# Scan inputs: fp32 products replaced by three float32r products on split operands, the parts made by ScalarE and Pool

## The chip, the cores and the metric

The program runs on one core of one Trainium2 chip. The metric is the device time of one execution in microseconds. The kernel before takes 3812.51 us (median of 3 runs, 3805.7 to 3818.8). Engines are called by the names of the profile: PE is TensorE, ACT ScalarE, DVE VectorE, POOL GpSimd (Pool), SP SyncE.

## What is computed

A chain of four blocks over 4096 tokens of width 256: an attention, a mixture of experts, a selective scan and a quantised feed-forward. The change is in the stage that makes the scan's inputs. Cut to what it computes:

```python
xz = einsum('bld,de->ble', xn, w_in)               # 256 -> 1024
x_path, z_path = split(xz, 2, axis=-1)             # 512 and 512
x_path = silu(causal_conv4(x_path) + b_conv)       # called xc below
Bseq, Cseq = x_path @ w_b, x_path @ w_c            # 512 -> 16 each
delta = softplus(x_path @ w_delta + b_delta)       # 512 -> 512
# handed on: delta, delta * x_path, Bseq, Cseq, x_path, silu(z_path)
```

## The kernel before

Each block is a function with its own engine programs. The function here is `scan_inputs` (names begin with `si_` in the profile). It goes over 8 groups of 512 tokens (GN), channels on the partitions. For one group g:

- `product_xz`: PE makes 8 outputs n of 128 channels, each from 2 matmuls (k) of 128x128 weights and 512 columns, into three rotating banks `ps_xz`. ACT copies each out (`copy_xz`): n = 0 to 3 to `xp`, n = 4 to 7 to `z`. From n = 3 on a product waits for the copy three before it, because of the three banks.
- DVE convolves `xp` (`convolve`: 4 tap-0 operations and 12 multiply-adds of 512), ACT takes the sigmoid in three passes (`sigmoid_conv`), DVE multiplies (`make_xc`) to `xc`.
- `product_xc`: PE makes `ps_d` (4 outputs x 4 matmuls with `w_delta`) and `ps_bc` (4 matmuls with `w_bc`, 32 columns of weights).
- Softplus: ACT magnitudes (`magnitude`), DVE `positive` and `correction`, ACT `logarithm`, DVE `make_delta` (two operations) and `delta_x`.
- PE turns delta times x (`turn`), ACT copies it out (`copy_turned`), SP stores it. ACT and DVE also make the z gate (`sigmoid_z`, `make_zs`).

All engines run their own program in order and wait on semaphores. `run_stages(eng, GROUPS, (stage, behind), ...)` sets the order: in step s the engine runs each stage in the listed order for group s - behind. So a step of PE is `product_xc(s-1)`, `turn(s-2)`, `product_xz(s+1)`; a step of ACT is magnitudes(s-1), `copy_turned(s-2)`, `sigmoid_conv(s)`, `logarithm(s-1)`, `copy_xz(s+1)`, `store_bc(s-1)`, `sigmoid_z(s)`; one of DVE is `convolve(s)`, `halo(s+1)`, `make_zs(s-1)`, `positive(s-1)`, `correction(s-1)`, `make_xc(s)`, `make_delta(s-1)`, `delta_x(s-1)`. POOL has nothing in the stage but three memsets at its start.

Of the kernel before, what the change touches and what calls it, by code (L numbers as in the profile page):

```python
# [13 lines left out]
F32 = mybir.dt.float32  # L14
BF16 = mybir.dt.bfloat16
I32 = mybir.dt.int32
ALU = mybir.AluOpType
# [1729 lines left out]
def scan_inputs(nc, io, scratch):  # L1747
# [5 lines left out]
    with ExitStack() as ctx:  # L1753
        r = Room(nc, ctx, "si")
        w_in, w_delta = r.sb("w_in", [P, KC, 2 * DI]), r.sb("w_delta", [P, DT, DI])
        w_bc = r.sb("w_bc", [P, DT, 2 * NS])
# [3 lines left out]
        xn_t = r.sb("xn_t", [P, 2, KC, GN])  # L1760
        xp, z = r.sb("xp", [P, DT, HALO + GN]), r.sb("z", [P, 2, DT, GN])
        conv, sig_c, sig_z = (r.sb(n, [P, DT, GN]) for n in ("conv", "sig_c", "sig_z"))
        xc, zs = r.sb("xc", [P, 2, DT, GN]), r.sb("zs", [P, DT, GN])
        mag, one_e, log, pos = (r.sb(n, [P, DT, GN]) for n in ("mag", "one_e", "log", "pos"))
        val = r.sb("val", [P, 2, 2, DT, GN])
        dx_t, b_t = r.sb("dx_t", [P, DT, GT, P]), r.sb("b_t", [P, GT, 2 * NS])
        bc = r.sb("bc", [2 * NS, GN])
        XZ = 3
# [5 lines left out]
                 "corr_ready", "log_ready", "sum_ready", "delta_ready", "dx_ready", "dx_turned", "dx_copied", "bc_turned", "b_copied",  # L1774
                 "bc_ready", "bc_copied", "xc_stored", "zs_stored", "delta_stored", "dx_stored", "b_stored", "bc_stored")
# [6 lines left out]
        with nc.Block() as block:  # L1782
            @block.sync
            def _(sp):
                sp.dma_start(w_in[:, :, :], io["w_in"].rearrange("(k p) e -> p k e", p=P)).then_inc(s["loaded"], 16)
# [10 lines left out]
                def load(g, slot):  # L1796
                    if third_on(g):
                        sp.wait_ge(s["xz_ready"], (g - 1) * 2 * DT)
                    sp.dma_start(xn_t[:, slot, :, :], tiles(scratch.xn_t, g)).then_inc(xn_loaded[slot], 16)

                def store_zs(g, slot):
                    sp.wait_ge(s["zs_ready"], g + 1)
                    sp.dma_start(tiles(scratch.zs, g), zs[:, :, :]).then_inc(s["zs_stored"], 16)
# [5 lines left out]
                def store_delta(g, slot):  # L1809
                    sp.wait_ge(s["delta_ready"], g + 1)  # L1810
                    sp.dma_start(tiles(scratch.delta, g), val[:, slot, 0, :, :]).then_inc(s["delta_stored"], 16)
# [20 lines left out]

            @block.vector
            def _(dve):
                CONV = DT * TAPS - 1
                dve.wait_ge(s["loaded"], 4 * 16)
                dve.wait_ge(s["keep_set"], 3)
# [59 lines left out]
                def make_delta(g, slot):  # L1897
# [3 lines left out]
                    dve.tensor_tensor(log[:, :, :], log[:, :, :], mag[:, :, :], ALU.subtract).then_inc(s["sum_ready"], 1)  # L1901
# [1048 lines left out]
```

## Time and profile before

| | |
|---|---|
| runs, median | 3812.51 us |
| profiled execution, its own time | 3818.61 us |
| its span | 3816.9 us |
| stage `scan_inputs` in it | about 2335 to 2675 us of the span |
| busy in that stage (340 us) | PE 282.22, DVE 223.19, ACT 204.42, POOL 1.96 us |

Times of rows are counted in microseconds from the start of the span. One plain fp32 matmul of the program stands in the trace as two MATMUL records (256 records of `si_w_in` for 128 matmuls). A wait in brackets is idle time of that engine just before the row, and what ended it. PEclk is the clock that TensorE was granted (1.0 is 2.4 GHz, 0.5 is 1.2 GHz).

### The profile page before, as it was taken

To read this page: it belongs to the slowest core of one execution; us is meant where nothing else is said; L and a number is where in the kernel's file an instruction comes from. 1 tells how busy PE (TensorE), PEld (TensorE's weight loads), DVE (VectorE), ACT (ScalarE), POOL (GpSimd) and SP (SyncE) were. 2 spreads that over 40 slices of the span, in tenths; PEclk is the share of its full clock that TensorE was granted. 3 is DMA by queue.
4 is the path that set the end of the run, shared out by engine and by line. 5 is a ranking of instruction groups with operands and counts; after the bars stand their busy time and mean duration, and the time that the engine had idled before them with its cause. 6 is when DMAs were issued, how large, how long until landed. Compare 5 with 4: busy or idle time off the path is not lost. (4 is left out here: it accounts for less than half of the span.)

```text
span 3816.9 us, 87664 instructions
## 1 busy us (share of the span) xinstructions
PE 3298.5 (86%) x34938; PEld 1884.3 (49%) x34939; DVE 2927.6 (77%) x4552; ACT 2057.6 (54%) x2972; POOL 1173.3 (31%) x910
## 2 busy tenths in 40 slices
PE   4769999999999999968699775997799999747876
PEld 1433333333333333326466552343687787546665
DVE  5659999998999999706344254676699999868986
ACT  0316777776777777833011155665565766334553
POOL 0100000000000000005100270000799999747775
PEclk8868999998999999967899866998899999879998
DMA  1674023030303120043222253333543434211110
GB/s 55 220 187 47 13 42 46 8 48 6 48 4 49 20 34 5 5 154 118 79 65 64 75 160 117 112 124 133 138 132 116 133 116 134 90 57 50 55 33 17
DMA packets 221875, 296.93 MB, mean 78 GB/s; under 512 B 56377, under 2 KB 154946, under 8 KB 219842
## 3 DMA queue, kind: packets, MB, share of 16 engines
q1 hardware_dynamic: 204258, 258.24, 25.1%
q0 software_dynamic: 6144, 17.05, 1.4%
q10 hardware_dynamic: 11120, 16.62, 1.3%
q8 instruction: 260, 4.26, 0.5%
q14 instruction: 93, 0.76, 0.1%
HBM read 174.75 MB, written 116.47 MB: 76 GB/s over the span
## 5 line engine op out<-in xcount | busy, mean ns | idle before, releaser
L921 DVE TENSOR_REDUCE att_maxima<-att_ps_m 128x1 f32<-128x512 f32 x2048 | 1286.4, 684 | 90.8 <-PE att_ps_m L977 89.3
L876 ACT ACTIVATE att_probs<-att_ps_s 128x1024 f32<-128x1024 f32 x1024 | 1000.0, 1022 | 289.9 <-PE att_ps_o L1004 276.7
L1004 PE MATMUL att_ps_o<-att_probs,att_vs 128*32 128x256 f32 x8192 | 662.6, 396 | 4.8 <-ACT att_probs L876 0.6
L977 PE MATMUL att_ps_m<-att_ks,att_qs 48*128 48x512 f32 x2048 | 587.3, 515 | 29.3 <-DMA att_ks<-scratch_k 28.6
L2235 POOL TENSOR_TENSOR ss_ch<-ss_h,ss_c_rep 128x1024 f32<-128x1024 f32 x256 | 601.6, 2416 | 12.4 <-DVE ss_h L2322 12.4
L2354 PE MATMUL ss_ps_u<-ss_diag,ss_dx_t 128*32 128x128 f32 x16384 | 476.0, 275 | 28.1 <-DMA ss_dx_t<-scratch_dx_t 14.6
L2354 PEld LDWEIGHTS ss_ps_u<-ss_diag,ss_dx_t 128*32 128x32 f32 x16384 | 454.2, 111 | 84.8 <-issue 63.9
L977 PEld LDWEIGHTS att_ps_m<-att_ks,att_qs 48*128 48x128 f32 x2048 | 238.7, 189 | 477.0 <-DVE att_maxima L921 393.6
L992 PE MATMUL att_ps_s<-att_qs,att_ks 50*128 50x512 f32 x2048 | 456.7, 407 | 4.0 <-DMA att_qs<-att_m_parts 1.2
L2274 ACT ACTIVATE ss_decay<-ss_delta,ss_a_neg 128x1024 f32<-128x1024 f32 x256 | 293.9, 1148 | 232.1 <-DVE ss_h L2322 210.1
L1004 PEld LDWEIGHTS att_ps_o<-att_probs,att_vs 128*32 128x32 f32 x8192 | 163.0, 108 | 365.1 <-issue 342.3
L2322 DVE TENSOR_TENSOR_SCAN ss_h<-ss_decay,ss_ps_u 128x1024 f32<-128x1024 f32 x128 | 286.4, 2275 | 47.5 <-PE ss_ps_u L2354 38.3
L2322 DVE TENSOR_TENSOR_SCAN ss_h<-ss_decay,ss_carry,ss_ps_u 128x1024 f32<-128x1024 f32 x128 | 293.2, 2334 | 7.7 <-POOL ss_ch L2235 4.8
L992 PEld LDWEIGHTS att_ps_s<-att_qs,att_ks 50*128 50x128 f32 x2048 | 223.4, 190 | 25.0 <-ACT att_probs L876 20.8
L856 POOL TENSOR_TENSOR att_heads<-att_o_t,att_sums 128x256 f32<-128x256 f32 x32 | 19.9, 621 | 702.0 <-DVE att_sums L936 702.0
L849 POOL TENSOR_TENSOR att_m_parts<-att_m_t,att_m_parts 16x128 fp32r<-16x128 f32 x32 | 14.4, 449 | 682.8 <-ACT att_m_parts L896 682.8
L1457 ACT ACTIVATE ex_y<-ex_ps_y,ex_x 128x256 f32<-128x256 f32 x72 | 34.1, 474 | 301.7 <-PE ex_ps_y L1528 301.7
L1661 POOL DMA_INDIRECT mo_back<-scratch_sorted_y,moe_packed x64 | 61.2, 956 | 345.5 <-DMA mo_b_norm<-in_b_norm 318.8
L2036 PE MATMUL si_ps_xz<-si_xn_t,si_w_in 128*128 128x512 f32 x256 | 119.4, 622 | 35.1 <-ACT si_xp L1984 15.8
L2375 PE MATMUL ss_ps_y<-ss_ch,ss_sum_block 128*32 128x512 f32 x1024 | 124.7, 602 | 15.3 <-POOL ss_ch L2235 15.1
L1510 PE MATMUL ex_ps_h<-moe_w_w,ex_x_t 128*128 x288 | 137.2, 599 | 0.4 <-issue 0.4
L1528 PE MATMUL ex_ps_y<-moe_w_w,ex_hid_t 128*128 x576 | 136.1, 379 | 0.0
(391 smaller groups left out, 4472.6 us busy)
## 6 DMA issues: line engine op xcount, KB each, us to landing
ss_delta<-scratch_delta SPq DMA_DIRECT2D x256, 128.0 KB, 3.1
att_qs<-scratch_q SPq DMA_DIRECT2D x96, 128.0 KB, 9.3
att_ks<-scratch_k SPq DMA_DIRECT2D x96, 128.0 KB, 10.7
ex_x<-scratch_sorted_x SPq DMA_DIRECT2D x72, 132.0 KB, 2.1
scratch_sorted_y<-ex_y SPq DMA_DIRECT2D x72, 128.0 KB, 1.7
scratch_v<-qkv_v_ext SPq DMA_DIRECT2D x8, 1024.0 KB, 4.4
scratch_q<-qkv_parts SPq DMA_DIRECT2D x16, 512.0 KB, 5.3
scratch_k<-qkv_parts SPq DMA_DIRECT2D x16, 512.0 KB, 6.0
```

The source lines that it names most:

```text
L876: act.activation(probs[:, (2 * n + pair) % 4, :, :], ps_s[pair][:, :, :], ACT.Exp, scale=HD ** -0.5).then_inc(exp_done, 1)
L921: dve.tensor_reduce(maxima[:, j, at:at + 1], ps_m[plan.bank(key)][:, :], AX.X, ALU.max).then_inc(maxed, 1)
L977: pe.matmul(ps_m[plan.bank(key)][:, :], qs[own, s // QC % 2, s % QC, p, t * P:(t + 1) * P], ks[own, s // QC % 2, p, c * GN:(c + 1) * GN], ...
L992: mm = pe.matmul(ps_s[pair][:, e, :], ks[rows_of(e, 0, ROWS), st // QC % 2, pair, kt * P:(kt + 1) * P], qs[rows_of(e, 0, ROWS), st // QC % ...
L1004: mm = pe.matmul(ps_o[h * VW:(h + 1) * VW, cols], vs[st // QC % 2][:, kt, h * VW:(h + 1) * VW], probs[:, (2 * n + h // 2) % 4, h % 2, cols ...
L1510: mm = pe.matmul(ps_h[slot][:, :], x_t[:, slot, k, :], w1[:, bass.ds(e, 1), k, :].rearrange("p a f -> p (a f)"), start=k == 0, stop=k == K ...
L1528: mm = pe.matmul(ps_y[slot][:, 0, :], hid_t[:, slot, f, :], w2[:, bass.ds(e, 1), f, :].rearrange("p a c -> p (a c)"), start=f == 0, stop=f ...
L2235: pool.tensor_tensor(ch[:, w.n % (CH_GROUPS * DQ), :], h[:, w.n % H_SLOTS, :], c_rep[:, w.ng, :], ALU.mult).then_inc(s["ch_ready"], 1)
L2274: act.activation(decay[:, w.n % DECAYS, :], delta[:, w.delta % DELTAS, :], ACT.Exp, scale=a_neg[:, at:at + 1]).then_inc(s["decay_ready"], 1)
L2322: dve.tensor_tensor_scan(h[:, w.n % H_SLOTS, :], decay[:, w.n % DECAYS, :], ps_u[w.n % U_BANKS][:, :], start, ALU.mult, ALU.add).then_inc( ...
L2354: mm = pe.matmul(ps_u[w.n % U_BANKS][q * DSUB:(q + 1) * DSUB, j * P:(j + 1) * P], dx_t[:, w.part % 2, j, w.dq * DSUB:(w.dq + 1) * DSUB], d ...
L2375: mm = pe.matmul(ps_y[dq * DSUB:(dq + 1) * DSUB, cols], block[:, :], ch[:, group % CH_GROUPS * DQ + dq, cols], start=False, stop=group % N ...
```

## The change

Every matmul of `product_xz` and `product_xc` becomes three matmuls in float32r, over `SPLIT = ((0, 0), (0, 1), (1, 0))`: high weights by high data, high by low, low by high. The high part is the value copied to float32r by ACT (`high_xn`, `high_xc`), the low part is value minus high, by POOL for the data (`low_xn`, `low_xc`) and by DVE for the weights, once (`split_low`). `high_xc` stands between the copies of `copy_xz` for the next group: one quarter before each of z's four copies. `product_xc` waits for all four quarters of both parts. To make room, zs is written over `sig_z`, the logarithm over `one_e` (so `logarithm` also waits for `corr_ready`), and delta times x has one buffer in place of two. Raw weights are loaded into the delta buffer.

```diff
@@ pool
+                def low_of(out, value, high):
+                    return pool.tensor_tensor(out, value, high.bitcast(F32), ALU.subtract)
+                def low_xn(g, slot):
+                    pool.wait_ge(s["xn_split"], g + 1)
+                    low_of(xn_t[:, slot, :, :], xn_t[:, slot, :, :].bitcast(F32), xn_high[:, :, :]).then_inc(s["xn_rest"], 1)
+                def low_xc(g, slot):
+                    for k in range(DT):
+                        pool.wait_ge(s["xc_split"], g * DT + k + 1)
+                        if k == 0 and not first(g):
+                            pool.wait_ge(s["bc_ready"], g)
+                        low_of(xc_low[:, k, :], xc[:, slot, k, :], xc_high[:, k, :]).then_inc(s["xc_rest"], 1)
+                run_stages(pool, GROUPS, (low_xc, 0), (low_xn, -2))
@@ vector
+                for part in range(W_PARTS):
+                    cols = slice(part * 2 * DI // W_PARTS, (part + 1) * 2 * DI // W_PARTS)
+                    dve.wait_ge(s["w_in_high"], part + 1)
+                    split_low(dve, w_in[1][:, :, cols], w_in_raw[:, :, cols], w_in[0][:, :, cols]).then_inc(s["w_in_low"], 1)
+                dve.wait_ge(s["w_second_high"], 2)
+                for w, raw in ((w_delta, w_delta_raw), (w_bc, w_bc_raw[:, :, :])):
+                    split_low(dve, w[1][:, :, :], raw, w[0][:, :, :]).then_inc(s["w_second_low"], 1)
@@ scalar
+                def high_xn(g, slot):
+                    act.wait_ge(xn_loaded[slot], (g // 2 + 1) * 16)
+                    if not first(g):
+                        act.wait_ge(s["xz_ready"], g * 2 * DT)
+                    act.activation(xn_high[:, :, :], xn_t[:, slot, :, :].bitcast(F32), ACT.Copy).then_inc(s["xn_split"], 1)
+                def high_xc(g, slot, k):
+                    if k == 0:
+                        act.wait_ge(s["xc_ready"], g + 1)
...
+                    act.activation(xc_high[:, k, :], xc[:, slot, k, :], ACT.Copy).then_inc(s["xc_split"], 1)
...
+                    act.wait_ge(s["corr_ready"], g + 1)
+                    act.activation(one_e[:, :, :], one_e[:, :, :], ACT.Ln).then_inc(s["log_ready"], 1)
 
                 def copy_xz(g, slot):
                     act.wait_ge(s["halo_set"], g + 1)
                     for n in range(2 * DT):
                         o = n % DT
+                        if o < n and (not isinstance(g, int) or g > 0):
+                            high_xc(g - 1, (slot - 1) % 2, o)
                         act.wait_ge(s["xz_ready"], g * 2 * DT + n + 1)
...
-                           (logarithm, 1), (copy_xz, -1), (store_bc, 1), (sigmoid_z, 0))
+                           (logarithm, 1), (copy_xz, -1), (last_high_xc, 0), (next_high_xn, -2), (store_bc, 1), (sigmoid_z, 0))
@@ tensor
                 def product_xz(g, slot):
-                    pe.wait_ge(xn_loaded[slot], (g // 2 + 1) * 16)
+                    pe.wait_ge(s["xn_split"], g + 1)
+                    pe.wait_ge(s["xn_rest"], g + 1)
...
                         for k in range(KC):
-                            mm = pe.matmul(ps_xz[n % XZ][:, :], w_in[:, k, n * P:(n + 1) * P], xn_t[:, slot, k, :], start=k == 0, stop=k == KC - 1)
+                            for i, j in SPLIT:
+                                mm = pe.matmul(ps_xz[n % XZ][:, :], w_in[i][:, k, n * P:(n + 1) * P], xn[j][:, k, :],
+                                               start=(k, i, j) == (0, 0, 0), stop=(k, i, j) == (KC - 1, *SPLIT[-1]))
...
                 def product_xc(g, slot):
...
-                    pe.wait_ge(s["xc_ready"], g + 1)
+                    pe.wait_ge(s["xc_split"], (g + 1) * DT)
+                    pe.wait_ge(s["xc_rest"], (g + 1) * DT)
```

ACT's program in the step that makes the sigmoid of group 1 (`si_sig_c`), before the loop of the later steps begins. Before:

```order
L1975 ACTIVATE si_log<-si_one_e 128x2048
L1984 ACTIVATE si_xp<-si_ps_xz 128x512 x4
L1984 ACTIVATE si_z<-si_ps_xz 128x512 x4
L1991 ACTIVATE si_bc<-si_ps_bc 32x512
L1993 DMA scratch_bc<-si_bc 32x512
L1929 ACTIVATE si_sig_z<-si_z 128x2048
```

The same place with the change:

```order
L2024 ACTIVATE si_one_e<-si_one_e 128x2048
L2036 ACTIVATE si_xp<-si_ps_xz 128x512 x4
L1965 ACTIVATE si_xc_high<-si_xc 128x512
L2036 ACTIVATE si_z<-si_ps_xz 128x512
L1965 ACTIVATE si_xc_high<-si_xc 128x512
L2036 ACTIVATE si_z<-si_ps_xz 128x512
L1965 ACTIVATE si_xc_high<-si_xc 128x512
L2036 ACTIVATE si_z<-si_ps_xz 128x512
L1965 ACTIVATE si_xc_high<-si_xc 128x512
L2036 ACTIVATE si_z<-si_ps_xz 128x512
L1956 ACTIVATE si_xn_high<-si_xn_t 128x1024
L2043 ACTIVATE si_bc<-si_ps_bc 32x512
```

Each copy of z now has a quarter of `xc_high` ahead of it, and the high part of the next `xn` follows the last.

POOL had nothing between the stage's memsets and the next stage. With the change its program from the last memset on, and into the loop over the later steps, is (the REGISTER_ALU rows only count the semaphores' values):

```order
L1836 MEMSET si_keep 128x2
L1839 TENSOR_TENSOR si_xn_t<-si_xn_t,si_xn_high 128x1024 x2
L173 UNCONDITIONAL_BRANCH
L173 ISA
L1839 TENSOR_TENSOR si_xc_low<-si_xc,si_xc_high 128x512
L1847 REGISTER_ALU
L1839 TENSOR_TENSOR si_xc_low<-si_xc,si_xc_high 128x512
L1847 REGISTER_ALU
L1839 TENSOR_TENSOR si_xc_low<-si_xc,si_xc_high 128x512
L1847 REGISTER_ALU
L1839 TENSOR_TENSOR si_xc_low<-si_xc,si_xc_high 128x512
L1842 REGISTER_ALU
L1839 TENSOR_TENSOR si_xn_t<-si_xn_t,si_xn_high 128x1024
```

The four quarters of `xc_low` are queued ahead of the low part of the `xn` of two groups later. DVE's program in a step keeps its order; ahead of the first step it has six new operations, the low parts of the weights.

## Rows read from the trace of the kernel before

**Rows 1.** The page's head: span and number of instructions.
```profile
span 3816.9 us, 87664 instructions
```

**Rows 2.** Busy time by engine over the whole stage, then granted clock, DMA share, GB/s.
```profile
2335.00:2675.00 340.00, 282.22 (x736) 123.34 (x736) 223.19 (x224) 204.42 (x232) 1.96 (x3) 0.93 0.34 120
```

**Rows 3.** Groups by line in the stage: count, busy, mean ns, idle before.
```profile
L2036 PE MATMUL si_ps_xz<-si_xn_t,si_w_in 128*128 128x512 f32 x256 | 119.4, 622 | 35.1 <-ACT si_xp L1984 15.8 <-DMA si_xn_t<-scratch_xn_t 15.6 <-ACT si_b_t L1962 2.9
```

**Rows 4.** Timeline of PE: start, length, operation, count, idle before. Groups 3, 5, 6.
```profile
2442.27 10.55 PE L2036 MATMUL si_ps_xz<-si_xn_t,si_w_in 128*128 128x512 f32 x20 [2.48 <-ACT si_xp L1984]
...
2519.00 8.85 PE L2036 MATMUL si_ps_xz<-si_xn_t,si_w_in 128*128 128x512 f32 x20 [2.49 <-ACT si_xp L1984]
2527.68 13.90 PE L2047 MATMUL si_ps_d<-si_xc,si_w_delta 128*128 128x512 f32 x32
2541.51 3.62 PE L2052 MATMUL si_ps_bc<-si_xc,si_w_bc 128*32 128x512 f32 x8
2545.06 1.53 PE L2018 MATMUL si_ps_xz<-all_ident,si_val 128*128 128x128 f32 x12
...
2556.51 8.85 PE L2036 MATMUL si_ps_xz<-si_xn_t,si_w_in 128*128 128x512 f32 x20 [2.48 <-ACT si_xp L1984]
```

**Rows 5.** Timeline of ACT at the same place, then a 128x512 group of ACT.
```profile
2516.57 1.89 ACT L1975 ACTIVATE si_log<-si_one_e 128x2048 f32<-128x2048 f32 x1
2518.37 1.55 ACT L1984 ACTIVATE si_xp<-si_ps_xz 128x512 f32<-128x512 f32 x3
2521.02 0.60 ACT L1984 ACTIVATE si_xp<-si_ps_xz 128x512 f32<-128x512 f32 x1 [1.09 <-PE si_ps_xz L2036]
...
L1942 ACT ACTIVATE si_mag<-si_mag 128x512 f32<-128x512 f32 x32 | 20.2, 630 | 1.0
```

**Rows 6.** Timeline of DVE at the same place.
```profile
2518.90 2.29 DVE L1901 TENSOR_TENSOR si_log<-si_log,si_mag 128x2048 f32<-128x2048 f32 x1
2521.39 2.29 DVE L1907 TENSOR_TENSOR si_val<-si_log,si_pos 128x2048 f32<-128x2048 f32 x1 [0.20 <-DVE si_log L1901]
2523.80 2.29 DVE L1913 TENSOR_TENSOR si_val<-si_val,si_xc 128x2048 f32<-128x2048 f32 x1
2526.01 1.91 DVE L1854 TENSOR_SCALAR si_conv<-si_xp,si_w_conv,si_b_conv 128x512 f32<-128x512 f32 x4
2527.96 8.29 DVE L1858 SCALAR_TENSOR_TENSOR si_conv<-si_xp,si_w_conv,si_conv 128x512 f32<-128x512 f32 x12
```

**Rows 7.** Timeline of PE in the feed-forward, whose products are split already.
```profile
3420.70 0.39 PE L2860 MATMUL fp_ps_gu<-fp_gate_up_t_high,fp_xq_t_low 128*128 128x512 f32 x1
...
3422.77 0.39 PE L2860 MATMUL fp_ps_gu<-fp_gate_up_t_high,fp_xq_t_low 128*128 128x512 f32 x1
```

**Rows 8.** DVE and POOL at once in two other stages: timeline, then min/median/max ns.
```profile
2298.46 2.35 POOL L1650 TENSOR_TENSOR mo_y<-mo_y,mo_ln_g 128x1024 f32<-128x1024 f32 x1 [14.10 <-ACT mo_y L145]
2300.53 1.35 DVE L1632 TENSOR_TENSOR mo_x<-mo_v,mo_x 128x1024 f32<-128x1024 f32 x1 [4.12 <-ACT mo_v L145]
2300.95 3.14 POOL L1654 TENSOR_TENSOR mo_v<-mo_y,mo_ln_b 128x1024 f32<-128x1024 f32 x1
...
L1632 DVE TENSOR_TENSOR mo_x<-mo_v,mo_x x8: 1225/1354/4066, 2201.8 to 2310.6; 128x1024 f32<-128x1024 f32 x8
L2742 POOL TENSOR_TENSOR fp_x_round<-fp_x_round,fp_x_magic x32: 715/724/909, 3395.0 to 3742.9; 128x256 f32<-128x256 f32 x32
L2414 DVE TENSOR_SCALAR fp_x_magic<-fp_x_round x16: 426/990/1048, 3393.3 to 3736.4; 128x512 int32<-128x512 int32 x16
```

**Rows 9.** The last group: PE's product and DVE's operation that it waits for.
```profile
2629.07 2.29 DVE L1895 TENSOR_TENSOR si_xc<-si_conv,si_sig_c 128x2048 f32<-128x2048 f32 x1 [7.57 <-ACT si_sig_c L1933]
2631.42 16.89 PE L2047 MATMUL si_ps_d<-si_xc,si_w_delta 128*128 128x512 f32 x32 [8.50 <-DVE si_xc L1895]
```

**Rows 10.** The stage's first product on PE.
```profile
2345.67 16.40 PE L2036 MATMUL si_ps_xz<-si_xn_t,si_w_in 128*128 128x512 f32 x32 [15.59 <-DMA si_xn_t<-scratch_xn_t]
```

More of the change, by code:

```diff
@@ L1754, in scan_inputs @@
         r = Room(nc, ctx, "si")
-        w_in, w_delta = r.sb("w_in", [P, KC, 2 * DI]), r.sb("w_delta", [P, DT, DI])
-        w_bc = r.sb("w_bc", [P, DT, 2 * NS])
+        w_in, w_delta, w_bc = ([r.sb(f"{n}_{half}", shape, F32R) for half in ("high", "low")]
+                               for n, shape in (("w_in", [P, KC, 2 * DI]), ("w_delta", [P, DT, DI]), ("w_bc", [P, DT, 2 * NS])))
         w_conv, b_conv, b_delta = r.sb("w_conv", [P, DT, TAPS]), r.sb("b_conv", [P, DT]), r.sb("b_delta", [P, DT])
@@ L1998, in sigmoid_z, with last_high_xc, next_high_xn @@
                         act.wait_ge(s["zs_ready"], g)
+                        act.wait_ge(s["zs_stored"], (g + 1) * 16)
                     sigmoid(sig_z[:, :, :], z[:, slot, :, :], "sig_z_steps", g * 2, "sig_z_ready")
+                def last_high_xc(g, slot):
+                    if isinstance(g, int) and g == GROUPS - 1:
+                        for k in range(DT):
+                            high_xc(g, slot, k)
+                def next_high_xn(g, slot):
+                    if not first(g):
+                        high_xn(g, slot)
                 run_stages(act, GROUPS, (first_magnitudes, 1), (last_magnitudes, 1), (copy_turned, 2), (sigmoid_conv, 0),
[L2002 removed]
+                           (logarithm, 1), (copy_xz, -1), (last_high_xc, 0), (next_high_xn, -2), (store_bc, 1), (sigmoid_z, 0))
             @block.tensor
@@ L2046, in product_xc @@
                         for k in range(DT):
-                            mm = pe.matmul(ps_d[o][:, :], w_delta[:, k, o * P:(o + 1) * P], xc[:, slot, k, :], start=k == 0, stop=k == DT - 1)
+                            for i, j in SPLIT:
+                                mm = pe.matmul(ps_d[o][:, :], w_delta[i][:, k, o * P:(o + 1) * P], xc_parts[j][:, k, :],
+                                               start=(k, i, j) == (0, 0, 0), stop=(k, i, j) == (DT - 1, *SPLIT[-1]))
                         mm.then_inc(s["d_ready"], 1)
@@ L2051, in product_xc @@
                     for k in range(DT):
-                        mm = pe.matmul(ps_bc[:, :], w_bc[:, k, :], xc[:, slot, k, :], start=k == 0, stop=k == DT - 1)
+                        for i, j in SPLIT:
+                            mm = pe.matmul(ps_bc[:, :], w_bc[i][:, k, :], xc_parts[j][:, k, :],
+                                           start=(k, i, j) == (0, 0, 0), stop=(k, i, j) == (DT - 1, *SPLIT[-1]))
                     mm.then_inc(s["bc_ready"], 1)
```

67 lines of the change are left out of this document (42 added, 25 removed).

## Prediction

> **What bounds the kernel now.** I read the page first [rows 1], then the busy times of the stage [rows 2]: of its 340 us PE works 282, DVE 223, ACT 204, POOL 2. PE is the engine to look at, but is it the limit? The groups by line say that its products with `w_in` were preceded by 35.1 us of idle time in all, 15.6 of it the load at the start and 15.8 a wait for ACT's `si_xp` [rows 3]. The timeline of PE shows where [rows 4]: from one start of product n = 3 to the next, 2519.00 to 2556.51, a period is 37.51 us. It is made of n = 3 to 7 (8.68), `ps_d` (13.83), `ps_bc` (3.55), and 11.45 from the end of `ps_bc` to the next n = 3. The last piece holds the turning, n = 0 to 2 and a wait of 2.48. That wait ends when ACT has made the logarithm and the first copy [rows 5]; ACT comes there from the turned block through three sigmoid passes. So these 11.45 us are set by ACT's chain: faster products n = 0 to 2 only lengthen the wait. The other 26.06 us are PE's own.
>
> **Price of the new products.** A plain fp32 product of 128x512 takes 8.68/10 = 0.868 us by n = 3 to 7 (10 products) and 13.83/16 = 0.864 in `ps_d` [rows 4]. The feed-forward runs the same split: from 3420.70 to 3422.77 are nine records, 0.230 us each [rows 7], so three make 0.69. A period's own PE work becomes 10 x 0.69 = 6.9, 16 x 0.69 = 11.0 and 4 x 0.69 = 2.8 (I take the narrow weights of `ps_bc` at the same price, as before they cost 0.89 each). Alone this would save 5.4 us a period.
>
> **What the parts cost.** ACT gets four 128x512 copies (0.63 each by its nearest group) [rows 5] and one of 1024, some 3.6 us a period. They stand where ACT was waiting 1.09 us for each product, and ACT is busy 204 of 340 us [rows 2]. PE's next wait for ACT is `ps_d`'s magnitudes, which do not hold PE up. I cost them at nothing, except the last quarter's delay, which is inside the chain below; without that cover they would cost 3.6 us a period, 22 us in six. The logarithm's new wait for `corr_ready` is nothing: the sigmoid passes stand between.
>
> POOL gets four subtractions of 512 and one of 1024. By its records of 256 (0.715) and 1024 (2.35) [rows 8] one of 512 takes 0.715 + 256 x 2.13 ns = 1.26 us. They have to be finished before `ps_d` may start, and the question is what DVE does at that time. Two rows decide it [rows 8]: DVE's `mo_x`, two inputs in SBUF, takes 1.23 at best and 4.07 at worst, and POOL's `mo_v` took 3.14 in place of 2.35, since it started at 2300.95 while `mo_x` ran until 2301.88; from there it took 2.21, its own time less 0.14. So such operations do not overlap but for 0.14 us. A DVE operation with one source in its fast form is hit too (0.426 at best, 0.990 in the median). The page "SBUF — State Buffer" of the Trainium skill (Who interferes with whom) says the same of GpSimd and a DVE operation with two SBUF inputs, the later one blocks until the first is done; the trace agrees but for the 0.14. By its exclusion for the whole instruction the sum would be 5 us higher, a part of rival D.
>
> **The chain before ps_d**, counted from the start of n = 3. DVE's subtraction and addition for delta stand at -0.10 to 2.19 and 2.39 to 4.68, delta times x is asked for at 4.80, tap 0 follows, then the multiply-adds at 0.69 each [rows 6]. PE ends n = 3 at 1.38; the copy begins 0.31 after (2521.02 less 2519.00 less 1.71 in the row) and takes 0.60, the first high quarter is ready at 2.9. POOL's first low quarter waits for DVE's addition until 4.68 and ends at 5.80. Delta times x, asked before that, runs until 7.96. The second quarter, ready to go at 5.8, ends at 9.08. The third runs beside tap 0 (no second source) until 10.34, one multiply-add slips in until 10.95, the fourth ends at 12.07. PE would be ready at 6.9. It starts `ps_d` at 12.1: a wait of 5.2 us which did not exist.
>
> **Sum.** New period: 12.1 + 11.0 + 2.8 + 11.45 = 37.35 against 37.51. Nearly the whole gain of 5.4 is eaten by the wait; five periods lie between n = 3 of groups 2 and 7, -1 us. Behind DVE's delay (6.7 us of POOL a period, with 27.9 of DVE's own) there is still room in 37 us; its next product, `xc`, waits 7.6 us for the sigmoid [rows 9].
>
> The start: after the load that PE waits for [rows 10], xn's high part (some 1.1) and its low part by POOL (2.35) stand ahead of the first product, 3.5 us; the weights' parts run beside them, but `w_delta`'s low part by DVE (2.29) stands ahead of `halo`, on which the first copy waits. From there to n = 3 of group 2 there are two more chains like the above, one with `ps_d` behind it, and shorter products. +4 us.
>
> The end: group 7 has no `product_xz` after it, so nothing hides its split. Before, PE starts `ps_d` 0.06 us after `si_xc` is finished [rows 9]. Now come 0.7 for the first quarter, and DVE is at its delta operations (three of 2.29, then zs), with POOL in turn: the first low quarter ends at 3.3, the second at 6.5, the third at 9.8, the fourth at 11 or 13, depending on whether `zs` goes first. I take 12. Around it: n = 3 to `ps_d` +3.4, and `ps_d` with `ps_bc` of groups 6 and 7 each -3.6. +8 us.
>
> The clock: equal 20 records took 10.55 and 8.85 [rows 4], both after a wait of 2.48; the first stretch was at 1.2 GHz for part of it, +1.7. Of five such waits in steady periods one was followed so. `ps_d` of the last group after 8.50 idle took 16.89 against 13.90, +3.0 [rows 4, 9]. Now each period has two longer waits, 3.8 and 5.2 us. A slow n = 3 to 7 is hidden under the chain of quarters; a slow `ps_d` is not. With 0.8 for each of six, less the 1.7 paid before: +3 us, between 0 and +13 (six times 3.0, less 1.7, were every one as the last, is 16; the shorter waits make that an outer bound).
>
> In all +4 - 1 + 8 + 3 = +14 us. The profiled execution took 3818.6 with a span of 3816.9 [rows 1], so 3832.6; it lies 6.1 over the median of 3812.5, to which I add the same 14: 3826, 0.4% slower.
>
> **The rivals.** (A) POOL's subtractions run beside DVE's, or find gaps. Then the quarters follow ACT's at 1.26 each, the last is done 1.4 after n = 7, the period is 8.3 + 11.0 + 2.8 + 11.45 = 33.55, five give -20, the end is -2 (5.7 for four quarters, -3.6 twice, -0.4), the start +1, the clock +3: -18, 3794. Speaks for it: ACT and POOL have the time. Against: [rows 8], in two stages. It decides in between: with the last quarter at 9.5 instead of 12.1 five periods give -13 and the sum is about zero. Chance 0.18.
>
> (B) The exchange is about as exclusive, but cheaper, since DVE's next operation does not always go first, or the clock costs nothing and the end takes 11: between -9 and +11, say 3816. Chance 0.29.
>
> (C) My forecast, +11 to +20. Chance 0.36.
>
> (D) The exchange costs more: no overlap at all, not even the 0.14 [rows 8], at some six exchanges a period (+0.8, 5 us in six periods), the chain's multiply-adds also alternate one for one, so that conv comes late for the sigmoid and DVE sets the period, and a slow `ps_d` each time: +20 to +32, 3839. For it: 27.9 + 6.7 us of DVE and POOL in turn are already 34.6 of 37.4. Chance 0.17.
>
> A measurement of this kernel can tell about 0.3%, 11 us. Slower is C and D, 0.53 (the line passes just under C); the same is B, 0.29; faster is A, 0.18. The range reaches from 3797, into A, to 3843, past most of D; C and its neighbours alone would be 3816 to 3835.
>
> **What would show it.** In the new profile: records of 0.23 us in both products; a wait of PE before `ps_d` of about 5 us a period on POOL's `xc_low`; POOL records of 512 columns of 2 to 3 us where 1.26 is their own, and DVE's delta times x at some 3.2; a period near 37.4; a wait ahead of the last `ps_d` near 20 us (8.5 before). If POOL's records are 1.26 and the wait about 1.4, (A) holds. The prediction is wrong too if a float32r product on these tiles is not 0.23, or if PE keeps 2.4 GHz throughout.

## The result, and the profile after

The changed kernel takes 3826.98 us (median of 8 runs, 3818.1 to 3847.25), the kernel before on the same chip 3812.46 (8 runs, 3804.23 to 3824.64). The ratio is 1.0051, with a 95% interval of 1.0033 to 1.007: slower by 14.5 us, half a per cent. The forecast was +14 and 3826.

Which part of the program has it? In the profiled executions the stage of the scan's inputs, from its first instruction to the first of the scan itself, took 338.8 us before (2335.44 to 2674.25) and 356.0 after (2329.42 to 2685.43): +17.2. The rest is the same code and lies 10 us the other way between these two executions. So where the time went is read from the stage, and what it is worth in the whole from the medians. A length of the stage is that of one profiled execution; two kernels that were profiled a second time gave 329.3 and 328.7, 314.5 and 314.3.

Busy time by engine over the stage after, the row that answers to [rows 2]:

```profile
2329.42:2685.43 356.01, 246.80 (x1024) 185.89 (x1024) 273.44 (x230) 234.42 (x278) 92.24 (x43) 0.87 0.32 115
```

PE works 35 us less than before, as it was meant to, and the stage is longer. POOL has 92 us where it had 2, DVE 273 where it had 223, although DVE got only the weights' low parts to do (some 7 us). What PE waited for instead, in the view of waits (total, times, longest):

```profile
PE si_ps_d L2119 <- issue: 28.1, 3, 21.7
PE si_ps_xz L2103 <- ACT si_xp L2036: 21.9, 7, 3.5
PE si_ps_xz L2103 <- DVE si_w_in_low L205: 19.9, 1, 19.9
PE si_ps_d L2119 <- POOL si_xc_low L1839: 18.9, 5, 5.0
```

The first and the fourth did not exist in that form: five waits before `ps_d` are put down to POOL's `xc_low`; the profile finds no releaser for three more ("issue"), among them that of the last group, 21.7. The groups by line show POOL and DVE stretched (busy, mean ns):

```profile
L1886 DVE SCALAR_TENSOR_TENSOR si_conv<-si_xp,si_w_conv,si_conv 128x512 f32<-128x512 f32 x96 | 73.0, 823 | 0.8
L1839 POOL TENSOR_TENSOR si_xc_low<-si_xc,si_xc_high 128x512 fp32r<-128x512 f32 x32 | 69.9, 2216 | 200.4 <-ACT si_xc_high L1965 200.4
L1882 DVE TENSOR_SCALAR si_conv<-si_xp,si_w_conv,si_b_conv 128x512 f32<-128x512 f32 x32 | 44.2, 1435 | 2.4 <-ACT si_xp L2036 2.4
L1940 DVE TENSOR_TENSOR si_dx<-si_delta,si_xc 128x2048 f32<-128x2048 f32 x8 | 25.2, 3152 | 0.3
```

POOL's subtraction of 512 has a mean of 2.22 us; DVE's delta times x has 3.15 where it took 2.29 [rows 6], and tap 0, which took 1.91 for four [rows 6], is at 1.44 each. The timeline of one period shows them taking turns: DVE, then POOL, the rows of POOL read one at a time.

```profile
2559.11 2.29 DVE L1928 TENSOR_TENSOR si_one_e<-si_one_e,si_mag 128x2048 f32<-128x2048 f32 x1
2561.59 2.29 DVE L1934 TENSOR_TENSOR si_delta<-si_one_e,si_pos 128x2048 f32<-128x2048 f32 x1 [0.19 <-DVE si_one_e L1928]
2563.91 3.28 DVE L1940 TENSOR_TENSOR si_dx<-si_delta,si_xc 128x2048 f32<-128x2048 f32 x1
2567.12 6.91 DVE L1882 TENSOR_SCALAR si_conv<-si_xp,si_w_conv,si_b_conv 128x512 f32<-128x512 f32 x4
2574.06 8.29 DVE L1886 SCALAR_TENSOR_TENSOR si_conv<-si_xp,si_w_conv,si_conv 128x512 f32<-128x512 f32 x12
```

```profile
2563.22 1.82 POOL L1839 TENSOR_TENSOR si_xc_low<-si_xc,si_xc_high 128x512 fp32r<-128x512 f32 x1 [28.77 <-ACT si_xc_high L1965]
2565.01 3.35 POOL L1839 TENSOR_TENSOR si_xc_low<-si_xc,si_xc_high 128x512 fp32r<-128x512 f32 x1
2568.32 1.46 POOL L1839 TENSOR_TENSOR si_xc_low<-si_xc,si_xc_high 128x512 fp32r<-128x512 f32 x1
2569.72 1.46 POOL L1839 TENSOR_TENSOR si_xc_low<-si_xc,si_xc_high 128x512 fp32r<-128x512 f32 x1
2571.14 2.60 POOL L1839 TENSOR_TENSOR si_xn_t<-si_xn_t,si_xn_high 128x1024 fp32r<-128x1024 f32 x1
```

POOL's first quarter is asked for at 2563.22 and ends 1.2 us after DVE's addition; delta times x, asked for at 2563.91, ends 3.28 later; the second quarter ends 1.2 behind that. Then tap 0's first three operations take some 1.5 each, as do the last two quarters, and its fourth, which meets POOL's low part of `xn`, takes 2.6: one of POOL for one of DVE. `ps_d` starts at 2571.28, 12.17 after n = 3.

From n = 3 of group 2 to n = 3 of group 7 lie five steady periods. The last table has a row of busy times for n = 3 to 7 and one for `ps_d` of four of them; the third figure from the end is the granted clock. These rows answer to [rows 4].

```profile
2438.97:2447.80 8.83, 8.83 (x30) 6.71 (x30) 8.60 (x5) 5.40 (x10) 5.29 (x2) 0.81 0.64 238
2451.26:2465.25 13.99, 13.99 (x49) 11.05 (x50) 13.61 (x17) 9.01 (x9) 2.29 (x1) 0.80 0.01 4
2479.26:2488.07 8.81, 8.80 (x30) 6.69 (x30) 8.59 (x5) 5.40 (x10) 5.84 (x2) 0.81 0.63 238
2491.56:2505.86 14.30, 14.30 (x49) 11.24 (x50) 13.93 (x18) 8.94 (x9) 2.28 (x1) 0.78 0.00 1
2519.87:2527.16 7.29, 7.29 (x30) 5.57 (x30) 7.05 (x4) 5.41 (x10) 4.38 (x2) 1.00 0.60 226
2532.17:2545.07 12.90, 12.90 (x49) 10.22 (x50) 12.52 (x16) 7.48 (x8) 2.29 (x1) 0.88 0.00 0
2559.11:2567.93 8.82, 8.82 (x30) 6.71 (x30) 8.60 (x5) 5.40 (x10) 4.71 (x2) 0.81 0.63 238
2571.28:2582.75 11.47, 11.47 (x49) 9.14 (x50) 11.29 (x16) 8.88 (x9) 2.46 (x1) 1.00 0.01 2
```

Read the starts first: `ps_d` comes 12.29, 12.30, 12.30 and 12.17 us after n = 3 (12.04 and 11.91 in the periods before and behind these), whether n = 3 to 7 took 7.29 or 8.83. So it is not the end of n = 3 to 7 that sets the start of `ps_d`. Then the lengths: `ps_d` takes 11.47 at 2.4 GHz throughout (granted 1.00) and 12.90 to 14.30 where part of it ran at 1.2 GHz (0.78 to 0.88), each time behind a wait of 3.5 to 5.0 us.

### The profile page after: what moved, and what is told of

Same layout as the page of the kernel before. It is cut to its first block and busy times, and to the rows that moved or that the text cites. A ratio compares the mean times of both kernels' runs of the same rounds, so it can differ in the third digit from the quotient of the medians.

```text
span 3824.0 us, 88405 instructions
## 1 busy us (share of the span) xinstructions
PE 3251.3 (85%) x35226; PEld 1946.0 (51%) x35227; DVE 2968.4 (78%) x4558; ACT 2090.3 (55%) x3018; POOL 1262.2 (33%) x950
## 5 line engine op out<-in xcount | busy, mean ns | idle before, releaser
L2429 PE MATMUL ss_ps_u<-ss_diag,ss_dx_t 128*32 128x128 f32 x16384 | 475.9, 275 | 26.2 <-DMA ss_dx_t<-scratch_dx_t 14.3
L1457 ACT ACTIVATE ex_y<-ex_ps_y,ex_x 128x256 f32<-128x256 f32 x72 | 34.2, 475 | 297.9 <-PE ex_ps_y L1528 297.9
L2450 PE MATMUL ss_ps_y<-ss_ch,ss_sum_block 128*32 128x512 f32 x1024 | 125.0, 602 | 14.5 <-POOL ss_ch L2310 14.2
L1839 POOL TENSOR_TENSOR si_xc_low<-si_xc,si_xc_high 128x512 fp32r<-128x512 f32 x32 | 69.9, 2216 | 200.4 <-ACT si_xc_high L1965 200.4
```

The lines of the kernel that those rows point to most:

```text
L2429: mm = pe.matmul(ps_u[w.n % U_BANKS][q * DSUB:(q + 1) * DSUB, j * P:(j + 1) * P], dx_t[:, w.part % 2, j, w.dq * DSUB:(w.dq + 1) * DSUB], d ...
L2450: mm = pe.matmul(ps_y[dq * DSUB:(dq + 1) * DSUB, cols], block[:, :], ch[:, group % CH_GROUPS * DQ + dq, cols], start=False, stop=group % N ...
```

## The experiments

Two statements were to be tested. T1: POOL's subtractions and DVE's operations take turns; that lengthens the chain to `ps_d`, and it eats what the products save. C1: what is lost beyond that is the clock after PE's waits. Nine kernels were run, two of them twice, in three sets (four, four and three rows of the table), each set on one chip beside the kernel before, whose medians there were 3811.18, 3813.66 and 3811.92. The changed kernel was not run again in these sets: it is compared by its ratio of 1.0051. All lengths of the stage are from the profiled executions, beside 338.8 before and 356.0 after.

| kernel | median us | ratio to before, 95% | stage us |
|---|---|---|---|
| POOL: memsets for xc's low parts | 3805.42 | 0.9975 (0.9954 to 0.9996) | 336.2 |
| xc's low parts by DVE | 3792.63 | 0.9949 (0.9927 to 0.997) | 329.3 |
| `product_xz` alone in two parts | 3802.64 | 0.9972 (0.9957 to 0.9987) | 335.1 |
| changed, 14 products ahead of `ps_d` | 3814.16 | 1.001 (0.999 to 1.0029) | 349.3 |
| changed, POOL's quarters twice | 3888.44 | 1.0189 (1.0146 to 1.0232) | 410.7 |
| `product_xz` alone, 14 products ahead of n = 3 | 3809.45 | 0.9974 (0.9949 to 0.9998) | 329.2 |
| low parts by DVE, 14 products ahead of n = 3 | 3796.24 | 0.9952 (0.9934 to 0.9971) | 317.9 |
| the same, last group's low parts first | 3788.63 | 0.9931 (0.9911 to 0.9952) | 314.5 |
| changed, the end in order | 3819.33 | 1.0017 (0.9997 to 1.0036) | 348.9 |
| low parts by DVE, again | 3800.07 | 0.9983 (0.9964 to 1.0002) | 328.7 |
| last group's low parts first, again | 3782.92 | 0.9934 (0.9913 to 0.9954) | 314.3 |

**The exclusion taken away.** POOL fills `xc_low` by a memset instead of the subtraction, behind an idle memset that keeps its time; the low part of xc is left out of the result. The edit also makes each quarter wait for the one before and unrolls POOL's loop.

```diff
-                        low_of(xc_low[:, k, :], xc[:, slot, k, :], xc_high[:, k, :]).then_inc(s["xc_rest"], 1)
+                        pool.wait_ge(s["xc_rest"], g * DT + k)
+                        pool.memset(idle[:, :], 0.0)
+                        pool.memset(xc_low[:, k, :].bitcast(F32), 0.0).then_inc(s["xc_rest"], 1)
...
-                run_stages(pool, GROUPS, (low_xc, 0), (low_xn, -2))
+                run_stages(pool, GROUPS, (low_xc, 0), (low_xn, -2), unroll=True)
```

> The changed kernel, with Pool's four subtractions for xc_low replaced by memsets of about the same length that read nothing (one of 700 columns beside, then one of 512 into xc_low; so the low parts of xc are zero: that part of the computation is left out). Semaphores and order stay. Theory T1 (Pool's subtraction and VectorE's operations of two SBUF inputs exclude each other): delta times x is back at 2.29 us, Pool's quarter takes its 1.2 us, TensorE's wait before ps_d falls from 3.1-5.0 us to about 1.5, the period from 37.6-40.6 to 33.5-35 and the stage from 356 to 320-330 us; the time lies at 3790 to 3802. Rival T2 (what delays ps_d is the length of Pool's own work and the hops from engine to engine, not the exclusion): waits and time stay within 3 us of the changed kernel.

The two memsets together take 1.38 us in the mean, more than a subtraction's own 1.25. Yet the wait before `ps_d` fell to 1.6 to 2.0 us, delta times x is back at 2.29, and the stage is 19.8 us shorter than the changed kernel's: 9.6 of it in the five steady periods, 9.5 at the end. The groups by line:

```profile
L1852 POOL MEMSET si_idle<- 128x700 f32 x32 | 23.7, 740 | 207.6 <-ACT si_xc_high L1968 206.1
L1885 DVE TENSOR_SCALAR si_conv<-si_xp,si_w_conv,si_b_conv 128x512 f32<-128x512 f32 x32 | 23.3, 784 | 2.5 <-ACT si_xp L2039 2.4
L1853 POOL MEMSET si_xc_low<- 128x512 f32 x32 | 20.4, 637 | 0.0
L1943 DVE TENSOR_TENSOR si_dx<-si_delta,si_xc 128x2048 f32<-128x2048 f32 x8 | 18.3, 2292 | 0.3
```

So POOL's time as such is not what holds `ps_d` up, and DVE's delta times x, with two sources, does not mind a POOL operation that only writes. But tap 0 still has 0.78 where it had 0.54. Its rows show why: POOL's memsets take turns with it and not with delta times x.

```profile
2559.66 2.29 DVE L1943 TENSOR_TENSOR si_dx<-si_delta,si_xc 128x2048 f32<-128x2048 f32 x1
2561.87 3.09 DVE L1885 TENSOR_SCALAR si_conv<-si_xp,si_w_conv,si_b_conv 128x512 f32<-128x512 f32 x4
```

```profile
2560.68 0.68 POOL L1852 MEMSET si_idle<- 128x700 f32 x1 [1.07 <-ACT si_xc_high L1968]
2561.30 0.53 POOL L1853 MEMSET si_xc_low<- 128x512 f32 x1
2562.09 0.94 POOL L1852 MEMSET si_idle<- 128x700 f32 x1 [0.26 <-ACT si_xc_high L1968]
2562.98 0.80 POOL L1853 MEMSET si_xc_low<- 128x512 f32 x1
```

The first pair runs beside delta times x (2559.66 to 2561.95) at 0.68 and 0.53, the second beside tap 0 at 0.94 and 0.80. T1 stands. But the expected gain was too large: the periods are 36.1 to 37.9 us (33.5 to 35 expected), the stage 336.2 (320 to 330), the whole 3 us above its range. The six `ps_d` from group 1 to group 6 took 13.0 in four cases, at a granted clock of 0.87, and n = 3 to 7 took 8.8 in every one: the clock again, here also behind waits before `ps_d` of only 1.8 to 2.0 us.

**POOL's time doubled.** Every quarter is made twice, the first time into a spare tile.

```diff
...
+                        low_of(spare[:, :], xc[:, slot, k, :], xc_high[:, k, :]).then_inc(s["spare_done"], 1)
+                        pool.wait_ge(s["spare_done"], g * DT + k + 1)
                         low_of(xc_low[:, k, :], xc[:, slot, k, :], xc_high[:, k, :]).then_inc(s["xc_rest"], 1)
```

> The changed kernel, but POOL makes each 512-column subtraction for xc_low twice, the first time into a spare tile (with a semaphore between the two). T1 (POOL and DVE take turns, and the wait before ps_d is POOL's quarters): four more subtractions of 1.26 us or more in the chain, and up to four more turns of DVE's multiply-adds (0.69 each): from n = 3 to ps_d 17 to 20 us in place of 12.2, the wait before ps_d 8 to 12 us, the period 44 to 47 us, tap 0 and the first multiply-adds of conv stretched to 1.5 to 2 us; the whole about +35 to +50 us over the changed kernel, 3855 to 3875. Rival T4 (the quarters are late by their hand-over from ACT and by semaphores, POOL's own time does not count): the chain stays at 12 to 14, the whole +0 to +12, 3818 to 3838.

From n = 3 to `ps_d` it is now 18.1 to 18.5 us, the wait 9.3 to 11.0, the period 45.3 to 46.6. Four subtractions of 1.26 are 5.0 of the 6.1 us more; the rest are turns. DVE at the same place:

```profile
2561.86 3.26 DVE L1943 TENSOR_TENSOR si_dx<-si_delta,si_xc 128x2048 f32<-128x2048 f32 x1
2565.04 5.74 DVE L1885 TENSOR_SCALAR si_conv<-si_xp,si_w_conv,si_b_conv 128x512 f32<-128x512 f32 x4
2570.82 13.31 DVE L1889 SCALAR_TENSOR_TENSOR si_conv<-si_xp,si_w_conv,si_conv 128x512 f32<-128x512 f32 x12
```

The multiply-adds went from 8.29 to 13.31: they are now the ones that POOL takes turns with. The rival (late by hand-over, not by POOL's time) falls: from n = 3 to `ps_d` it would have stayed at 12 to 14. The whole is above the expected range by 13 us, since I had counted the steady periods alone: the stage's start grew by 8 and its end by 14 on top of 33 in five periods.

**The exclusion avoided.** DVE makes the quarters itself, between delta and delta times x.

```diff
-                run_stages(pool, GROUPS, (low_xc, 0), (low_xn, -2))
+                run_stages(pool, GROUPS, (low_xn, -2))
...
-                           (correction, 1), (make_xc, 0), (make_delta, 1), (delta_x, 1))
+                           (correction, 1), (make_xc, 0), (make_delta, 1), (low_xc, 0), (delta_x, 1))
```

> The changed kernel, with the low parts of xc made by VectorE instead of Pool, between make_delta and delta_x. T1: without the exclusion four operations of 0.69 follow the addition for delta; the last waits for the last high quarter, at 7.1 to 8.6 us from the start of n = 3, so ps_d starts at about 8.0 to 9.4 in place of 12.2; period 33.2 to 34.6, the last ps_d starts 7.3 after si_xc in place of 13.2, stage 318 to 326 us, time 3790 to 3800. Rival T3 (VectorE has no room: its 27.9 us a period and 2.8 more make it the limit): the sigmoid waits for the convolution and the period stays at 37 or more.

DVE takes 0.69 us for a quarter where POOL takes 1.25 alone and 2.22 in turn. The wait before `ps_d` is 0.6 to 0.7, `ps_d` takes 11.5 in every steady period, and the stage is 26.7 us shorter than the changed kernel's. Yet the stage (329.3, 318 to 326 expected) and the periods (35.1 to 36.2, 33.2 to 34.6 expected) are longer than T1 alone said, and `ps_d` starts 9.5 to 10.6 us after n = 3, not 8.0 to 9.4: n = 3 to 7 takes 8.8 to 10.0 in every one, behind waits of 3.6 to 4.9 us. T3 falls, since the period did not stay at 37. Two measurements against the kernel before give 0.9949 and 0.9983 (the second is outside the 0.993 to 0.997 that was expected for it, and its interval just reaches 1.0002), both below the changed kernel's 1.0051. The quarters on DVE take back the loss of the change; that this kernel is faster than the kernel before is shown by the first measurement and not by the second.

**One product alone.** `product_xz` in two parts, `ps_d` and `ps_bc` in plain fp32 (the edit takes out all that concerns xc's parts and the second weights).

```diff
-                            for i, j in SPLIT:
-                                mm = pe.matmul(ps_d[o][:, :], w_delta[i][:, k, o * P:(o + 1) * P], xc_parts[j][:, k, :],
-                                               start=(k, i, j) == (0, 0, 0), stop=(k, i, j) == (DT - 1, *SPLIT[-1]))
+                            mm = pe.matmul(ps_d[o][:, :], w_delta_raw[:, k, o * P:(o + 1) * P], xc[:, slot, k, :], start=k == 0, stop=k == DT - 1)
```

> Only product_xz is split into three float32r products; product_xc stays plain fp32 on xc, so xc needs no parts. By the terms of the sum: n = 3 to 7 take 6.9 instead of 8.68, all else of the period stays, so 35.75 against 37.51, five periods give -9, the start costs +1, the end nothing: stage 331 us, time 3804 (faster by 0.2%). Rival T2': if the parts of xn (ScalarE 1.05, Pool 2.35 against VectorE's tap 0) cost something on the path, the period stays at 37.

The gain in the steady periods did not come: 37.4 to 37.5 us in four of five, as before. The wait before n = 3 is 3.44 instead of 2.48, since n = 0 to 2 are faster; behind each of the five waits of 3.44 n = 3 to 7 took 8.8, and 7.29 at 2.4 GHz behind the one wait of 1.46, in the one period of 36.0. What the product saved there, the clock took back. The median, 3802.6, is what was expected (3804), but not for the reason given: the stage is 335.1 where 331 was expected. Two of the five:

```profile
2507.36:2516.19 8.83, 8.82 (x31) 7.04 (x32) 8.60 (x8) 3.33 (x6) 0.00 (x0) 0.81 0.63 238
2544.87:2553.69 8.82, 8.82 (x31) 7.05 (x32) 8.59 (x8) 3.32 (x6) 0.00 (x0) 0.81 0.63 238
```

**PE kept busy ahead of n = 3.** The same kernel, with products into a free bank that nobody reads.

```diff
+                        if n == XZ and third_on(g):
+                            pe.wait_ge(s["pos_ready"], (g - 2) * DT + 1)
+                            for _ in range(14):
+                                pe.matmul(ps_d[0][:, :], w_in[0][:, 0, 0:P], w_in[0][:, 0, 0:GN], start=True, stop=True)
                         if n >= XZ:
```

> The kernel with only product_xz in two parts (ps_d and ps_bc plain fp32), and 14 products that nobody reads put into PE's idle time ahead of n = 3, which fill its wait of 3.44 us. C1 (the saving of product_xz was lost to the clock after that wait): n = 3 to 7 takes 7.3 us in each steady period in place of 8.8, the period 35.9 to 36.3 in place of 37.5, the stage 7 to 10 us shorter than in the kernel without them, the whole 3793 to 3797 on this chip if it stood at 3803. C2 (the slow stretch has nothing to do with the idle time before it): n = 3 to 7 stays at 8.8, period 37.5, same time.

Now n = 3 to 7 takes 7.29 in every steady period, and the period is 35.9:

```profile
2509.51:2516.79 7.28, 7.28 (x31) 5.91 (x32) 7.05 (x5) 3.32 (x6) 0.00 (x0) 1.00 0.60 226
2545.47:2552.76 7.29, 7.29 (x31) 5.92 (x32) 7.06 (x5) 3.32 (x6) 0.00 (x0) 1.00 0.61 224
```

Five periods became 6.2 us shorter, the stage 5.9 (7 to 10 expected). C1 is shown for this stretch, in the trace. In the whole time it does not appear: 0.9974 against 0.9972, a comparison that is uncertain by 0.0029, some 11 us.

**The same before `ps_d`.** In the changed kernel 14 unread products stand ahead of `product_xc`'s wait for the parts.

```diff
+                    if not first(g):
+                        pe.wait_ge(s["pos_ready"], (g - 1) * DT + 1)
+                        for _ in range(14):
+                            pe.matmul(ps_d[0][:, :], w_delta[0][:, 0, 0:P], w_delta[0][:, 0, :], start=True, stop=True)
                     pe.wait_ge(s["xc_split"], (g + 1) * DT)
                     pe.wait_ge(s["xc_rest"], (g + 1) * DT)
```

> The changed kernel, with 14 unused float32r products of 512 columns (3.2 us at full clock) into ps_d's first bank before the wait for the parts of xc, which the real product then overwrites. Theory C1 (TensorE's idle 3.1 to 5.0 us before ps_d lowers its clock, and that costs the path): ps_d takes 11.5 us in every period where it took 13.0 to 14.3 in four of six, stage shorter by 8 us, time 3819. Rival C2 (the slow clock is repaid elsewhere, or the waits before n = 3 alone cause it): ps_d stays at 13 to 14 in most periods, or the time stays within 2 us of the changed kernel.

`ps_d` took 11.5 in the steady periods, the period is 37.4 to 38.5 where it was 37.6 to 40.6, the stage is 6.7 us shorter, and the ratio 1.001 in place of 1.0051. The wait for the quarters is still there, only filled for the most part with unread work. So of the stage's +17.2 some 7 are the clock. The ratios differ by 0.0041, uncertain by 0.0027: 5 to 26 us in unprofiled runs too.

**Both repairs, and the end.** DVE makes the quarters, PE has the unread products ahead of n = 3; then, for the last group alone, the quarters are put ahead of delta's two operations.

```diff
...
-                           (correction, 1), (make_xc, 0), (make_delta, 1), (low_xc, 0), (delta_x, 1))
+                           (correction, 1), (make_xc, 0), (last_low_first, 0), (make_delta, 1), (low_xc, 0), (delta_x, 1))
```

In the last group `last_low_first` makes the four quarters and `low_xc` makes none.

> All three products in two parts, xc's low parts by DVE between delta and delta times x, and the 14 unread products ahead of n = 3. C1: n = 3 to 7 takes 7.3 to 8.2 us in place of 8.8 to 10.0. But DVE's low quarters wait for ACT's high quarters, which follow ACT's copies of n = 3 to 7, so the wait before ps_d becomes 1 to 2 us: the period 34.2 to 35 in place of 35.6 on average, the whole 4 to 8 us below the kernel without them (3792.6): 3785 to 3789. C2: same time as without.

> The one before, and for the last group alone DVE makes xc's low parts straight behind xc, ahead of delta's two operations (2.29 each). The wait before the last ps_d was 15.5 us with the low parts behind them; the four subtractions then end about 3.5 us behind xc in place of 7.4, so ps_d starts 4 us earlier. Theory (the end of the stage hangs on this chain): -3 to -4.5 us against the one before. Rival (what follows ps_d waits for DVE's delta of group 6 and its turning, which now comes 2.8 us later): -1 to +1.

With the unread products n = 3 to 7 is at 7.29 in place of 8.8 to 10.0 and the period 33.5 to 33.7, less than the 34.2 expected: the quarters kept up. The stage is 11.3 us shorter; the whole time, which was expected to fall by 4 to 8 us, did not show it (0.9952 against 0.9949, uncertain by 0.0028). With the quarters first the wait before the last `ps_d` fell from 15.48 to 11.74 and the stage by 3.4 more:

```profile
2607.14 0.77 PE L2131 MATMUL si_ps_d<-si_xc_high,si_w_delta_high 128*128 128x512 f32 x1 [11.74 <-issue]
```

Its whole time, -7.6 against the one before, is less certain than that (about 10 us). A set of its own settled whether the stage's gain is real outside a profile:

> The kernel with xc's low parts by DVE once more, for a comparison in more rounds on one chip with the next. Stage 329 us, ratio to before 0.993 to 0.997.

> The kernel with xc's low parts by DVE, the unread products ahead of n = 3 and the last group's low parts first, once more, in more rounds on one chip with the one before. C1 (the clock's loss is real in unprofiled runs too): by the stage in the profiles (329.3 against 314.6) 10 to 16 us below the kernel without these two edits. C2 (the gain shows in a profiled run alone, or other stretches of the program lose it again): within 4 us of it.

On one chip, 3800.07 and 3782.92: 0.9983 and 0.9934, a difference of 0.0049 with an uncertainty of 0.0028, 8 to 29 us where the stage says 14.3. These two kernels differ by both edits, and the stage gives 3.4 of the 14.3 to the second. So the gain of the two together is real outside a profile. The clock's share of it is made likely by this and by the unread products ahead of `ps_d`; the two comparisons in which the products ahead of n = 3 are the only difference do not show it. This version is 0.7% faster than the kernel before in both sets (0.9931 and 0.9934) and the fastest here. The rows of the second run, n = 3 to 7 and `ps_d` of one period:

```profile
2513.93:2521.21 7.28, 7.28 (x30) 5.56 (x30) 6.48 (x6) 5.39 (x10) 0.00 (x0) 1.00 0.62 233
2521.78:2533.26 11.48, 11.48 (x49) 9.15 (x50) 11.41 (x13) 10.64 (x12) 3.27 (x1) 1.00 0.20 68
```

**The tail of the change alone.** In the changed kernel DVE waits, in the last group only, until POOL has made all four quarters.

```diff
+                def let_last_parts_go(g, slot):
+                    if isinstance(g, int) and g == GROUPS - 1:
+                        dve.wait_ge(s["xc_rest"], GROUPS * DT)
...
-                           (correction, 1), (make_xc, 0), (make_delta, 1), (delta_x, 1))
+                           (correction, 1), (make_xc, 0), (let_last_parts_go, 0), (make_delta, 1), (delta_x, 1))
```

> The changed kernel with one wait more: in the last group alone DVE does not begin delta's operations of group 6 until POOL has made all four low quarters of group 7. T1 (the tail's +8 us is POOL's quarters in turn with DVE's three operations and zs, where delta's operations are wanted later than the quarters): the quarters take 1.26 us each, the last ends 5.8 us behind xc in place of 13.2, the wait before the last ps_d is 14 to 15 us in place of 21.7, the stage 7 us shorter (349 in place of 356), the whole -5 to -8 us against the changed kernel. Rival (POOL's records of 3.2 us are its own slowness in this stage, or the end hangs on the delta that is now 5.8 us late): POOL's records stay above 2 us or the wait before the last turning takes back what ps_d gains; the whole within 2 us of the changed kernel or slower.

The same four subtractions, first in the changed kernel, in turn with DVE's four, then here, with DVE held back:

```profile
2634.72 12.39 POOL L1839 TENSOR_TENSOR si_xc_low<-si_xc,si_xc_high 128x512 fp32r<-128x512 f32 x4 [26.22 <-ACT si_xc_high L1965]
```

```profile
2641.95 4.99 POOL L1839 TENSOR_TENSOR si_xc_low<-si_xc,si_xc_high 128x512 fp32r<-128x512 f32 x4 [26.19 <-ACT si_xc_high L1969]
```

12.39 against 4.99: four quarters at 1.25 each, the estimate of 1.26. The wait before the last `ps_d` fell from 21.69 to 14.27, the stage by 7.1, and the ratio from 1.0051 to 1.0017 (a difference of 0.0034, uncertain by 0.0027). A wait more on DVE made the kernel faster; the delta that now comes 5.8 us later is wanted later than that.

## Why the prediction was right, and which terms were off

**The products' price** held. `ps_d` takes 11.47 for 48 at 2.4 GHz, 0.239 each by the ends of its records, where 11.0 was put: +0.5 a period. n = 3 to 7 takes 7.29 (6.9).

**The chain before `ps_d`** held to 0.2 us: 12.1 was forecast, 11.91 to 12.30 measured. A wait of 5.2 was forecast; it is 3.1 to 5.0, since PE itself comes later where its clock was low. The doubled quarters (18.1 to 18.5) and the memsets (waits of 1.6 to 2.0) show the cause.

**One step of it was wrong, without effect on the sum.** "The third runs beside tap 0 (no second source) until 10.34, one multiply-add slips in until 10.95, the fourth ends at 12.07." Tap 0 is not free beside POOL: its four records took 6.91 in place of 1.91, and POOL's third and fourth quarters took turns with them. The trace of before had the sign of it: tap 0 takes 0.48 for 512 columns (1.91 for four) where a multiply-add takes 0.69 [rows 6], so it is in the fast form that the prediction itself called "hit too" by [rows 8]. They ended at 10.67 and 12.07 after n = 3, because a turn with tap 0 (some 1.4) cost about what I had put for the free quarter and for the multiply-add. That this came out at 12.1 was luck.

**The end**, +8 forecast: from n = 3 of group 7 to the next stage 80.30 became 88.75, +8.45. The quarters ended 3.3, 6.6, 9.9 and 13.1 after `si_xc`, by 3.3, 6.5, 9.8 and "11 or 13", and zs did go first. Holding DVE back gave 7.1 of it back.

**The start**, +4 forecast, +1.2 measured (first instruction to n = 3 of group 2: 69.30 and 70.47). Up to the first product it is +4.35, from 10.23 to 14.58, where 3.5 was worked out. That "the weights' parts run beside them" was wrong: DVE's first part of `w_in`, which reads two sources in SBUF, took its turn behind POOL's low part of `xn`, 2.35 us in place of 0.68, and the first product waited for it.

```profile
2340.95 2.36 POOL L1839 TENSOR_TENSOR si_xn_t<-si_xn_t,si_xn_high 128x1024 fp32r<-128x1024 f32 x1 [9.51 <-ACT si_xn_high L1956]
2341.50 2.35 DVE L205 TENSOR_TENSOR si_w_in_low<-si_delta,si_w_in_high 128x512 fp32r<-128x512 f32 x1 [22.98 <-ACT si_w_in_high L1971]
```

What I priced too high are the two chains behind it: group 0 has no delta of a group before it for POOL to take turns with, so `ps_d` of group 0 waited 2.2 us, not 5, and the faster products gave 3.2 back.

**The clock** was the mis-sized term. At full clock a steady period is 12.2 + 11.5 + 14.0 (`ps_bc`, turning, n = 0 to 2 and the wait for ACT) = 37.7, five of them 188.5. Before, five were 189.2, of which 1.7 went to the clock: 187.5. That is +1.0 by -1, for the most part the 0.5 a period of `ps_d`'s price. But `ps_d` was 1.4 to 2.8 us longer in four of five: 8.3 in all, less the 1.7 paid before, +6.6 where +3 stood for the whole stage. Together +7.6, as the five periods measured: 196.79 against 189.21. That a slow n = 3 to 7 would be hidden was right.

So +1.2 + 7.6 + 8.45 = +17.2 in this execution, by +14: the start was 3 too high, the products' price 2 and the clock 4 too low. That the medians lie 14.5 apart, as near to the forecast as this, is partly luck: an error of 3 one way stands against 6 the other way, and the difference of the medians is itself uncertain by 7 us. Of the rivals, A falls by the turns; B, the cheaper exchange, by the chain of 12.2. D's multiply-adds in turn came in the steady periods only with twice the quarters; in the changed kernel five of the 96 took a turn, all in the start.

## What to carry to other kernels

Before work is moved to an idle engine, look at what the busy engine beside it does in those microseconds: where DVE's operations there have two sources in SBUF, or one in the fast form of tap 0, their times and those of POOL's subtractions add up (3.28 for 2.29 and 1.5 for 0.54 here), and the idle engine's slower record is what the waiting one pays (2.22 here; 0.69 had the busy engine done it itself). Where such a pair meets once, at the end of a stage, a wait that puts the urgent one first can be worth more than the overlap (7 us here). And a saving on PE in a stretch between waits has to be read with the granted clock: shorter products leave longer waits, and the next stretch may give the gain back.

## What was not expected of the hardware

Tap 0, a DVE TENSOR_SCALAR in fp32 with one source and its result in SBUF, is held up by POOL as much as the operations with two sources: mean 543 ns before, 1435 after, in turn one for one, and by POOL's memsets too (784), which leave delta times x at 2.29. The page "SBUF — State Buffer" of the Trainium skill (Who interferes with whom) has both cases: `tensor_scalar` in a mode that uses two ports meets any GpSimd operation, an operation with two SBUF inputs only one that reads SBUF. The trace agrees with each; I had used the second half of the rule and not the first. That tap 0 is in such a mode is inferred from its speed; no run here shows the mode itself.

PE's clock stood at 1.2 GHz for part of n = 3 to 7 after five of five waits of 3.44 us (`product_xz` alone in two parts; four of five in the changed kernel), where after 2.48 us it was so in one of five [rows 4]. Over all traces it was so after 25 of 30 waits of 3.44 to 3.46 and after 3 of 10 of 2.46 to 2.49: the wait makes it more likely and does not decide it alone. With the wait filled it was at 2.4 GHz in all. The slow part cost 1.5 us on 7.3 behind waits of 3.44 us in these two kernels, and up to 2.8 elsewhere (10.04 with unread products ahead of `ps_d`).
